# Group attention of a decoder layer: four normalisations per step written on ScalarE in place of GpSimd

## The reference

```python
ln_out = _ln(hidden_states, ln_w, ln_b)
q = _fp8_linear_pertensor(ln_out, wq, wq_scale, q_in_scale).reshape(b, s, g, hpg, d)
q = _ln(q, qln_w, qln_b)
k = _ln(_fp8_linear_pertensor(ln_out, wk, wk_scale, k_in_scale).reshape(b, s, g, d), kln_w, kln_b)
v = _fp8_linear_pertensor(ln_out, wv, wv_scale, v_in_scale).reshape(b, s, g, d)
core = _gqa(q, k, v).reshape(b, s, nh * d)
qx = _ln(_fp8_linear_pertensor(ln_out, wqx, wqx_scale, qx_in_scale)...)
...
xout = _gqa(qx, kx, vx).reshape(b, s, nh * d)
catq = _div_clamp_fp8(jnp.concatenate([core, xout], axis=-1), proj_smooth)
return jnp.einsum('bsi,oi->bso', catq, wproj) * (proj_in_scale * proj_w_scale)
```

## Time and profile before

| | |
|---|---|
| time, median of 3 runs | 2484.04 us (2480.91 to 2487.3) |
| the profiled execution | 2486.31 us, span of its instructions 2484.5 us |
| mean granted PE clock | 0.966 of full speed |
| PE busy | 2317.3 us, 93% of the span |
| DVE busy | 1415.6 us, 57% |
| ACT busy | 1138.5 us, 46% |
| POOL busy | 1152.1 us, 46% |

### The profile page before, as it was taken

The page is one execution under the profiler, slowest core; times in us unless marked ns, Lnnn a source line. Parts: engine busy times, 40 slices in busy tenths (PEclk is TensorE's granted clock), DMA queues, the critical chain, the costliest instruction groups (busy, mean ns, idle before and its releaser), DMA issues. The chain is left out here.

```text
span 2484.5 us, 39824 instructions
## 1 busy us (share of the span) xinstructions
PE 2317.3 (93%) x14528; PEld 1308.1 (53%) x14528; DVE 1415.6 (57%) x2936; ACT 1138.5 (46%) x2165; POOL 1152.1 (46%) x1396
## 2 busy tenths in 40 slices
PE   6899888968999999999999859999999999999999
PEld 3566544535666666666666534444444444444444
DVE  5766687437999989999999852222222222222221
ACT  3455465447777778877778721111111111111110
POOL 2422327656787878778786324131313131313131
PEclk9799799979999999999999969999999999999999
DMA  4100012127878888888888741101010101010000
GB/s 151 35 19 18 1 60 103 76 102 158 157 149 164 155 167 162 159 155 154 166 151 150 138 152 73 68 34 68 34 68 34 68 34 67 35 67 35 0 0 34
DMA packets 437986, 224.81 MB, mean 90 GB/s; under 512 B 406224, under 2 KB 410320, under 8 KB 433616
## 3 DMA queue, kind: packets, MB, share of 16 engines
q1 hardware_dynamic: 415952, 186.74, 33.0%
q10 hardware_dynamic: 21888, 36.19, 5.6%
HBM read 103.34 MB, written 18.87 MB: 49 GB/s over the span
## 5 line engine op out<-in xcount | busy, mean ns | idle before, releaser
L1955 ACT ACTIVATE sil<-bank 128x512 f32<-128x512 f32 x128 | 76.4, 597 | 772.4 <-PE bank L301 772.4
L1928 POOL TENSOR_SCALAR hh<-h 128x512 f16<-128x512 f32 x128 | 105.1, 821 | 679.4 <-DVE h L2026 679.4
L2026 DVE TENSOR_TENSOR h<-bank,sil 128x512 f32<-128x512 f32 x128 | 88.6, 692 | 530.6 <-PE bank L301 422.8
L1572 ACT ACTIVATE xprob<-bank,xnm 128x1024 f32<-128x1024 f32 (+1 forms) x240 | 220.2, 917 | 185.2 <-DVE xnm L1663 185.0
L1675 DVE SCALAR_TENSOR_TENSOR xparts<-xprob,xri,xparts 128x1024 f16<-128x1024 f32 (+1 forms) x240 | 273.2, 1138 | 3.3 <-ACT xparts L1580 3.2
L1663 DVE TENSOR_REDUCE xnm<-bank 128x1 f32<-128x512 f32 (+1 forms) x256 | 242.9, 949 | 50.7 <-PE bank L301 49.3
L1580 ACT ACTIVATE xparts<-xprob,xri 128x1024 f16<-128x1024 f32 (+1 forms) x240 | 227.7, 949 | 0.0
L299 PE MATMUL bank<-eXTh,ewh_gate 128*128 128x512 f16 x512 | 194.8, 380 | 3.5 <-DVE ewl_gate L1973 3.5
L300 PE MATMUL bank<-eXTh,ewl_gate 128*128 128x512 f16 x512 | 194.8, 380 | 0.0
L301 PE MATMUL bank<-eXTl,ewh_gate 128*128 128x512 f16 x512 | 194.7, 380 | 0.0
L299 PE MATMUL bank<-eXTh,ewh_up 128*128 128x512 f16 x512 | 194.1, 379 | 0.0
(11 more groups left out here) (289 smaller groups left out, 5966.7 us busy)
## 6 DMA issues: line engine op xcount, KB each, us to landing
xkv<-kv_made ACTq DMA_DIRECT2D x64, 256.0 KB, 3.3
raw_gate<-in_gate SPq DMA_DIRECT2D x8, 2048.0 KB, 7.8
raw_up<-in_up SPq DMA_DIRECT2D x8, 2048.0 KB, 7.9
raw_down<-in_down SPq DMA_DIRECT2D x8, 2048.0 KB, 7.8
xwraw<-in_w_group ACTq DMA_DIRECT2D x60, 256.0 KB, 3.4
kv_made<-vst SPq DMA_DIRECT2D x16, 512.0 KB, 4.2
kv_made<-kst SPq DMA_DIRECT2D x16, 512.0 KB, 2.6
kvraw<-in_w_kvx SPq DMA_DIRECT2D x4, 1024.0 KB, 6.7
```

Source lines behind the costliest of these rows:

```text
L1572: act.activation(prob[prob_of(u)][:, 0:L], SC[u % 2][:, 0:L], ACT.Exp, bias=nm[:, u % 4:u % 4 + 1], accum_out=rs[:, u % 4:u % 4 + 1]).then ...
L1928: pool.tensor_scalar(hh[half][:, f, :], h[i % 2][:], 1.0, 1.0, ALU.mult, ALU.mult).then_inc(h_hi, 1)
L1955: act.activation(sil[i % 2][:], bank[:, 2 * (i % 2), :], ACT.Silu, scale=1.0 / WS).then_inc(silu, 1)
L2026: dve.tensor_tensor(h[i % 2][:], bank[:, 2 * (i % 2) + 1, :], sil[i % 2][:], ALU.mult).then_inc(made, 1)
```

## The change

ACT normalises, beside the keys (blocks 16 to 19), the blocks of the first query head (0 to 3). The key blocks stay in slot 11; the new four are done in slot 12, behind that slot's exponential and high part and ahead of the read of `T4`. POOL normalises blocks 4 to 15 instead of 0 to 15. PE's transpose `T0` waits for ACT's count instead of POOL's, and `T1` to `T3` wait for a POOL count that is four lower. The first heads, before the steps, are made as before (`ACT_APPLIES[:BT]`).

```diff
-ACT_APPLIES = range(4 * BT, 5 * BT)
-POOL_APPLIES = range(4 * BT)
+ACT_APPLIES = list(range(4 * BT, 5 * BT)) + list(range(BT))
+POOL_APPLIES = range(BT, 4 * BT)
...
-            def apply_keys(m):
+            def apply_first(m, blocks):
                 act.wait_ge(s_shift, m)
-                for i in ACT_APPLIES:
+                for i in blocks:
                     act.activation(norm_block(i), norm_block(i), ACT.Identity, scale=rstd[:, i:i + 1],
                                    bias=shift[:, i:i + 1]).then_inc(applied_act, 1)
...
-                    if u == 11 and not last:
-                        apply_keys(n + 1)
+                    if u in (11, 12) and not last:
+                        apply_first(n + 1, ACT_APPLIES[BT * (u - 11):BT * (u - 10)])
...
-                    if j == 4:
-                        after(pe, applied_act, BT * m)
+                    if j in (4, 0):
+                        after(pe, applied_act, len(ACT_APPLIES) * (m - 1) + BT * (1 + (j == 0)))
                     elif m:
-                        pe.wait_ge(applied, len(POOL_APPLIES) * (m - 1) + BT * (j + 1))
+                        pe.wait_ge(applied, len(POOL_APPLIES) * (m - 1) + BT * j)
```

More of the change, by code:

```diff
@@ L1104, in _ @@
                     act.wait_ge(f_shift, 1)
-                    for k in ACT_APPLIES:
+                    for k in ACT_APPLIES[:BT]:
                         act.activation(first_block(k), first_block(k), ACT.Identity, scale=frstd[:, k:k + 1],
```

## The result

| | before | after |
|---|---|---|
| median | 2485.28 us (4 runs) | 2505.65 us (4 runs, 2497.71 to 2507.61) |
| ratio | | 1.0079, 95% interval 1.0057 to 1.0101 |
| the profiled execution | span 2484.5 us | span 2502.6 us |

The changed kernel is 0.8% slower, 20 us by the medians and 18.1 us between the two profiled executions. A second set of six runs gave 2503.00 us beside 2486.22 us, ratio 1.0066 (1.0045 to 1.0088). The direction and the range of the forecast held; its likeliest value, 12.7 us, is too small by 4 to 8 us.

The account below looks back on a forecast made before the run. The prediction took PE as the bound, losing time only where it waits, for ACT's reads among others. From the median, 2484.0 + 12.7 us of ACT delay = 2496.7 us, 0.51% slower; range 2486 to 2507 us.

Parts of the forecast that it names:

- What bounds the stage: In one step, at full granted clock, PE is busy 51.86 of 54 us; it waits for ACT's `ft`, not POOL's blocks.
- ACT's price and cover: In slots 12 to 15, four instructions cost 1.53 us, of which 0.70 is covered: PE 0.83 us later a step.
- The cover of 0.70 us: ACT could have begun exponential 13 0.70 us earlier: it waited 0.60 us and starts 0.10 us before the read's end.
- Nothing given back: Later in the step, at PE's wait for `cat`, 0 of the 0.83 us delay is given back.
- POOL's head start at 0: POOL's four fewer normalisations, 2.5 us a step, are used up waiting for ACT's read at `T4`'s subtraction: gain 0.
- the first rival: Nothing absorbed: waits ahead of `T2`, `T3` stay, or a DVE low part falls behind POOL's subtraction; 23 us, 2507 us; chance 0.15.
- The sum: 14 steps at 0.83 = 11.6 us, with 1.10 us for step 0 12.7 us: 2496.7 us, 0.51% slower; chance 0.60.
- The wait for `cat` took up nothing: Rival: POOL or DVE holds `cat`, so PE waits 6 us less, or all 12.7; 2484 to 2491 us; chance 0.17.
- POOL's head start did not reach it: Rival: POOL's head start reaches `cat`, shortening the first wait of `Y0` in each step; 2473.5 us, faster; chance 0.08.

Follow-up runs that it names:

- POOL's part alone: Kernel before, POOL normalising only blocks 4 to 15 and nobody normalising the first head, PE's waits lowered to match: 2485.73 us, ratio 1.0003.
- eight instructions: Kernel before with eight more ACT instructions in slot 12, into a scratch tile nobody reads, POOL unchanged: 2543.32 us, ratio 1.0242.
- two blocks: Changed kernel with ACT normalising the keys and only two blocks of the first head, POOL the rest: 2489.08 us, ratio 1.0019 to the kernel before.
- `T0` filled: Changed kernel with PE making the scores of slot 14 twice, first ahead of `T0`: 2503.74 us, ratio 1.0064 to the kernel before.
- both edits: Kernel before with POOL's split of the first weights cut in two and slot 13's order turned round on ACT and DVE: 2479.31 us, ratio 0.9977.
- the wait for `cat` filled: PE runs overwritten matmuls ahead of `Y0`'s wait for `cat`: in the changed kernel 2493.28 us, the kernel before 2486.33 us, with both edits 2474.18 us.

## Why the prediction was right

*What bounds the stage.* Right. PE waited for ACT's reads, not for POOL's blocks, and POOL's part alone changed the time by 0.0003 of it, which is not told from 0.

*ACT's price and cover.* Right. Four instructions were put at 1.53 us and took 1.54; `T0` waits 1.62 us; the 0.60 us ahead of exponential 13 are gone; `T2` no longer waits and `T3` waits 0.19 us. 0.83 us a step was forecast; 0.80 us on PE was read in one step, and 0.82 a step over two without a fall. The cover of 0.70 us is borne out by eight instructions, 2.40 us a step against 2.36, and less exactly by two, 0.3 us a step against 0.07.

*Nothing given back.* Right: PE's wait for `cat` was 23.2 us and is 22.1.

*POOL's head start at 0.* Right for the change itself. With two blocks it is a small loss, 0.2 us in the step that was read, by the collision of `xkl` with DVE's low part that the first rival named for another pair of instructions.

*The sum.* Its waiting, 12.7 us, is confirmed by the trace, which has 12.2 us over 14 steps where the forecast's terms give 1.10 + 13 x 0.83 = 11.9, and by executions at like clocks (12 to 15 us). The step that failed is the first one: it took the granted clock of one undisturbed step (1.00) for that of the stage. The clock fell five times in six behind the waits for `cat`, before once in six: 6.8 us in the profiled executions, where 4 to 8 us were missing. The rivals had no such case. That the result lay in the range is in part luck: its upper end was made for a stall that is not absorbed at all, and it held the result for another reason.

*The rivals.* The one in which nothing is absorbed gives about the measured 20 us, and is wrong all the same: `T2` and `T3` took back 0.7 us in the step that was read, and the steps without a fall are 0.8 us longer, not 1.5. The wait for `cat` took up nothing, and POOL's head start did not reach it.

*Open.* Why the clock falls behind five of six nearly equal waits in one kernel and behind one of six in another was not found. The one without a fall in the changed kernel is the shortest of its six (2.35 us), but with `T0` filled one of 2.33 us has a fall, and in the kernel before four of 2.7 us have none. Nor is it the length of the step in a simple way: with two blocks, 110.2 us for two steps without a fall, the profiled execution has four of six, and with both edits, 108.2 us, it has four as well. In the profiled executions with the wait for `cat` filled there is none, so the waits are needed for these falls; what picks among them stays open.

## What to carry to other kernels

An engine that is busy for half of the time can have one short chain on which the bound engine waits; count its idle time between the first and the last link of that chain, not over the step. Here it was 0.60 us where the total said 11 of 54 us. And where TensorE has waits of 2 to 3 us, compare the granted clock right behind each of them before and after, over the whole stage, and not by its mean: an unchanged wait can cost more in a changed rhythm. Keeping TensorE busy in it can then be worth more than the work it adds, but in a kernel whose clock hardly falls it was worth nothing.

## What was not expected of the hardware

- Waits of 2.35 to 2.72 us on PE were followed by 3.4 us at half clock in one case of six in one kernel and in five of six in the other. Each fall made its step 1.7 us longer. In the second kernel, matmuls that fill the waits, 2.6 us of work without use, took the falls away and made it about 10 us faster; in the first they changed nothing.
- Shorter waits did not end the falls: in the version with both edits waits of 2.1 us were followed by one in four cases of six.
- A wait of 1.62 us was not followed by a fall in the stretches looked at; with 3.16 us at the same place there were falls at three steps in a row.
- An `xkl` of POOL begun 0.47 us ahead of a DVE instruction with two inputs in SBUF made that one 0.50 us longer, 1.77 us instead of 1.27; begun 0.21 us behind it, POOL's own took 2.08 us instead of 1.16.
